# One gather in 96 moved from GpSimd to row-by-row transfers of SyncE

## What is computed

```python
h = (x @ W).reshape(n_nodes, Hh, Cc)
a_src = (h * att_src).sum(-1)
a_dst = (h * att_dst).sum(-1)
alpha = leaky_relu(a_src[src] + a_dst[dst])
m = jax.ops.segment_max(alpha, dst, num_segments=n_nodes)
e = jnp.exp(alpha - m[dst])
denom = jax.ops.segment_sum(e, dst, num_segments=n_nodes)
w = e / jnp.clip(denom, 1e-16)[dst]
out = jax.ops.segment_sum(w[:, :, None] * h[src], dst, num_segments=n_nodes)
```

## Time and profile before

| | |
|---|---|
| runs | 9,905.91, 9,902.95, 9,856.30 us; median 9,902.95 |
| profiled execution | 9,816.89 us, its span 9,815.1 us, mean granted TensorE clock 0.685 |
| PE busy | 5,477.6 us (56%), weight loads 3,976.8 (41%) |
| DVE busy | 5,141.6 us (52%) |
| POOL busy | 4,917.7 us (50%) |
| ACT busy | 2,159.9 us (22%) |
| DMA | 996.05 MB, mean 101 GB/s; GpSimd's queue 23.5% of 16 engines, SyncE's 9.6%, ScalarE's 2.0% |

### The profile page before, as it was taken

The page is one execution under the profiler, slowest core; times in us unless marked ns, Lnnn a source line. Parts: engine busy times, 40 slices in busy tenths (PEclk is TensorE's granted clock), DMA queues, the critical chain, the costliest instruction groups (busy, mean ns, idle before and its releaser), DMA issues. The chain is left out here.

```text
span 9815.1 us, 109787 instructions
## 1 busy us (share of the span) xinstructions
PE 5477.6 (56%) x24127; PEld 3976.8 (41%) x24128; DVE 5141.6 (52%) x15278; ACT 2159.9 (22%) x4026; POOL 4917.7 (50%) x5343
## 2 busy tenths in 40 slices
PE   5565555565655555555555555665555555555551
PEld 4344343344444434444444344553334443343330
DVE  3455454455546545554554445665545554554559
ACT  4111111121112412112111111351111111111113
POOL 2455555455453445545544455564444444444446
PEclk7666666666677766666666666786666666666665
DMA  7333333333333433333333333353333333333333
GB/s 195 89 98 96 96 96 96 94 99 98 94 99 85 135 94 100 98 94 100 98 94 94 93 99 96 113 170 94 96 96 96 96 96 95 95 95 96 93 91 106
DMA packets 489012, 996.05 MB, mean 101 GB/s; under 512 B 147014, under 2 KB 298808, under 8 KB 488342
## 3 DMA queue, kind: packets, MB, share of 16 engines
q0 software_dynamic: 227376, 635.50, 23.5%
q1 hardware_dynamic: 190836, 292.76, 9.6%
q10 hardware_dynamic: 70514, 65.01, 2.0%
HBM read 922.29 MB, written 70.57 MB: 101 GB/s over the span
## 5 line engine op out<-in xcount | busy, mean ns | idle before, releaser
L928 POOL DMA_INDIRECT e_rows<-table,e_loaded x4704 | 4462.1, 949 | 4482.0 <-PE e_p_mm L1001 2591.5
L1001 PE MATMUL e_p_mm<-e_rows,e_onehot 128*128 128x264 f32 x9408 | 2678.8, 447 | 0.0
L1001 PEld LDWEIGHTS e_p_mm<-e_rows,e_onehot 128*128 128x128 f32 x9408 | 2055.1, 224 | 438.7 <-issue 12.4
L1123 DVE TENSOR_TENSOR e_rows<-e_rows,e_p_e 128x1024 f32<-128x1024 f32 x1176 | 1418.4, 1206 | 0.0
L974 ACT ACTIVATE e_rows<-e_gap 128x64 f32<-128x64 f32 (+1 forms) x294 | 80.5, 274 | 5578.1 <-DVE e_gap L1281 5578.1
L1212 DVE TENSOR_TENSOR_SCAN e_fwd<-e_mask,e_p_one 64x128 f32<-64x128 bf16 (+1 forms) x294 | 121.7, 414 | 2138.4 <-remote 1724.3
L1115 DVE TENSOR_TENSOR e_onehot<-e_col,e_p_iota 128x512 f32<-128x512 f32 (+1 forms) x1470 | 951.0, 647 | 301.6 <-issue 292.6
L1059 PE MATMUL e_p_small<-ident,e_fwd 64*1 64x64 f32 (+1 forms) x588 | 114.1, 286 | 1657.0 <-DVE e_bwd L1213 996.1
L994 PE MATMUL e_p_mm<-e_xmsg,e_onehot 128*128 128x264 f32 x1764 | 888.6, 674 | 13.8 <-issue 13.8
L1246 DVE TENSOR_REDUCE e_adst<-e_p_one 128x64 f32<-128x192 f32 (+1 forms) x294 | 122.7, 417 | 1447.1 <-remote 1447.1
L1008 PE MATMUL e_p_one<-ad_parts,e_onehotT 128*128 x5586 | 536.8, 183 | 408.8 <-issue 407.2
(11 more groups left out here) (213 smaller groups left out, 6359.5 us busy)
## 6 DMA issues: line engine op xcount, KB each, us to landing
e_onehotT<-rel_rows SPq DMA_DIRECT2D x294, 608.0 KB
e_rows<-table,e_loaded POOLq DMA_INDIRECT x4704
table<-n_row ACTq DMA_DIRECT2D x196, 130.0 KB, 2.9
n_looprow<-table SPq DMA_DIRECT2D x196, 128.0 KB, 2.6
table<-n_row ACTq DMA_DIRECT2D x98, 132.0 KB, 1.9
n_node<-in_x_pad SPq DMA_DIRECT2D x98, 128.0 KB, 3.1
e_mask<-mask_rows SPq DMA_DIRECT2D x196, 64.0 KB
n_resrow<-in_x_pad SPq DMA_DIRECT2D x98, 128.0 KB, 2.6
```

The source lines that it names most:

```text
L928: pool.indirect_dma_start(rows[k][:, g, 0:TW], None, table[L], bass.IndirectOffsetOnAxis(ap=idx[k][:, g:g + 1], axis=0)).then_inc(s_gat[k] ...
L1001: ins = nc.tensor.matmul(p_mm[:, bass.ds(region, MW)], onehot[:, g, :], rows[k][:, g, :], start=False, stop=True, skip_group_check=True)
L1123: return nc.vector.tensor_tensor(feats, feats, p_e[:, g4, :].unsqueeze(3).to_broadcast([P, 4, H, C]), ALU.mult)
```

## The change

One gather in 96 leaves GpSimd's stream. Windows are counted in turns of six (TURN). In the last window of a turn GpSimd issues 15 gathers, and the 128 rows of that window's tile 15 are fetched by SyncE: in each of the first five windows of the turn it loads up to 26 node numbers (DIRECT) into registers and issues one transfer per row into a buffer of its own (`direct`; in the third layer a part of `as32`). In the sixth it waits for all of them and for the row buffer to be free, and copies `direct` into `rows[k][:, 15]` by one transfer in SBUF. ScalarE waits for that copy before its compact. SyncE's column load is issued one window ahead, the node numbers come with one small load per turn, and GpSimd's, SyncE's and ScalarE's loops are unrolled by six instead of three; TensorE and VectorE are as they were.

```diff
@@ -48,12 +48,14 @@
 BUFS = 3
+TURN = 6
+DIRECT = 26
...
-REGION_ROW, AD_ROW, WINDOW_ROW = 0, 32, 64
+REGION_ROW, AD_ROW, WINDOW_ROW, SRC_ROW = 0, 32, 64, 96
@@ -821,7 +823,9 @@
+    s_direct = [sem(f"e_direct{k}") for k in range(2)]
+    s_nodes, s_placed = (sem(f"e_{n}") for n in ("nodes", "placed"))
...
@@ -841,6 +845,7 @@
+            direct = sbuf(ph, tag + "direct", [P, TW], F32)[:] if TOPS else as32[:, 0:TW]
@@ -868,28 +873,29 @@
-            def walk(engine, body):
+            def walk(engine, body, unroll=BUFS):
...
-                for w in range(BUFS):
-                    at(w, w, 1, first=w == 0)
-                with engine.Fori(1, WINDOWS // BUFS) as i:
-                    for k in range(BUFS):
-                        at(i * BUFS + k, k, i + 1)
-                for w in range(WINDOWS // BUFS * BUFS, WINDOWS):
+                for w in range(unroll):
+                    at(w, w % BUFS, w // BUFS + 1, first=w == 0, turn=(0, w))
+                with engine.Fori(1, WINDOWS // unroll) as i:
+                    for r in range(unroll):
+                        at(i * unroll + r, r % BUFS, i * (unroll // BUFS) + (r // BUFS + 1), turn=(i, r))
+                for w in range(WINDOWS // unroll * unroll, WINDOWS):
                     at(w, w % BUFS, w // BUFS + 1)
@@ -919,25 +925,41 @@
-                def body(w, k, turns, ago, first):
+                def body(w, k, turns, ago, first, turn):
                     pool.wait_ge(s_idx[k], turns * 16)
-
-                    for g in range(G):
+                    by_row = turn is not None and turn[1] == TURN - 1
+
+                    for g in range(G - 1 if by_row else G):
...
-                walk(pool, body)
+                walk(pool, body, TURN)
...
-                def body(w, k, turns, ago, first):
-                    wait_apart(sp, st["cols"], ago(BUFS))
+                def load_columns(w, k):
                     sp.dma_start(loaded[k][:], col_dram[:, bass.ds(w * COL_W, COL_W)]).then_inc(s_idx[k], 16)
+
+                def load_nodes(i):
+                    sp.dma_start(off_row[SRC_ROW:SRC_ROW + 1, 0:P],
+                                 t["src_rows"][bass.ds(i * (TURN * G) + (TURN * G - 1), 1), :]).then_inc(s_nodes, 16)
+
+                def load_direct(first_row, n):
+
+                    nodes = words(sp, SRC_ROW, first_row, n, NODES_PAD - 1)
+                    for p, node in enumerate(nodes, first_row):
+                        sp.dma_start(direct[p:p + 1, :], table[L][bass.ds(node, 1), :]).then_inc(s_direct[p % 2], 16)
+
+                def body(w, k, turns, ago, first, turn):
+                    if first:
+                        load_columns(0, 0)
+                    if turn is not None and turn[1] == 0:
+                        load_nodes(turn[0])
                     wait_apart(sp, st["settled"], ago(BUFS))
...
-                walk(sp, body)
+                    if not (isinstance(w, int) and w == WINDOWS - 1):
+                        wait_apart(sp, st["cols"], ago(BUFS - 1))
+                        load_columns(w + 1, (k + 1) % BUFS)
+                    if turn is None:
+                        return
+                    i, r = turn
+                    if r == 0:
+                        wait_apart(sp, s_nodes, count(sp, (i + 1) * 16))
+                        wait_apart(sp, st["compact"], ago(1))
+                    if r < TURN - 1:
+                        load_direct(r * DIRECT, min(DIRECT, P - r * DIRECT))
+                    else:
+                        for parity in range(2):
+                            wait_apart(sp, s_direct[parity], count(sp, (i + 1) * (P // 2 * 16)))
+                        wait_apart(sp, s_mm[3], ago(BUFS))
+                        sp.dma_start(rows[k][:, G - 1, 0:TW], direct).then_inc(s_placed, 16)
+                walk(sp, body, TURN)
@@ -959,11 +997,17 @@
...
-                    act.wait_ge(s_gat[k], turns * (16 * G))
+                    gathered = turns * (16 * G)
+                    if turn is not None and k == TURN % BUFS + BUFS - 1:
+                        i, r = turn
+                        gathered = i * (2 * 16 * G - 16) + (16 * G if r < TURN - 1 else 2 * 16 * G - 16)
+                        if r == TURN - 1:
+                            wait_apart(act, s_placed, count(act, (i + 1) * 16))
+                    act.wait_ge(s_gat[k], count(act, gathered))
...
-                walk(act, body)
+                walk(act, body, TURN)
```

More of the change, by code:

```diff
@@ L93, in build_program @@
     zeros = sbuf(top, "zeros", [1, G * ADS_W], BF16)
-    off_row = sbuf(top, "off_row", [WINDOW_ROW + 1, TILES], I32)
+    off_row = sbuf(top, "off_row", [SRC_ROW + 1, TILES], I32)
     as32 = sbuf(top, "as32", [P, BLOCKS * 8], F32)
@@ L823, in build_program @@
     s_turn, s_done, s_step = (sem(f"e_{n}") for n in ("turn", "done", "step"))
-    per_layer = [*s_idx, *s_ld, s_turn, s_done, s_step]
+    s_direct = [sem(f"e_direct{k}") for k in range(2)]
+    s_nodes, s_placed = (sem(f"e_{n}") for n in ("nodes", "placed"))
+    per_layer = [*s_idx, *s_ld, s_turn, s_done, s_step, *s_direct, s_nodes, s_placed]
     s_clear = sem("e_clear")
@@ L869, in edge_phase, with at @@
             flat = lambda a: a[:].rearrange("o h g -> o (h g)")
-            def walk(engine, body):
-                def at(w, k, turns, first=False):
+            def walk(engine, body, unroll=BUFS):
+                def at(w, k, turns, first=False, turn=None):
                     regs = {}
@@ L881, in ago @@
                         return regs[n]
+                    place = () if unroll == BUFS else (turn,)
                     if isinstance(w, int):
-                        body(w, k, turns, ago, first)
+                        body(w, k, turns, ago, first, *place)
                     else:
-                        body(w if engine is nc.gpsimd else engine.snap(w), k, engine.snap(turns), ago, first)
-                for w in range(BUFS):
-                    at(w, w, 1, first=w == 0)
-                with engine.Fori(1, WINDOWS // BUFS) as i:
-                    for k in range(BUFS):
-                        at(i * BUFS + k, k, i + 1)
-                for w in range(WINDOWS // BUFS * BUFS, WINDOWS):
+                        body(w if engine is nc.gpsimd else engine.snap(w), k, engine.snap(turns), ago, first, *place)
+                for w in range(unroll):
[4 more added lines that the diff above has]
+                for w in range(WINDOWS // unroll * unroll, WINDOWS):
                     at(w, w % BUFS, w // BUFS + 1)
@@ L1359 @@
         "x_pad": x_pad, "edge_rows": np.ascontiguousarray(edge_rows), "edge_cols": np.ascontiguousarray(edge_cols),
-        "dst_rows": dst_rows, "tile_ends": np.concatenate([tile_first, tile_base, tile_last])[None],
+        "dst_rows": dst_rows, "src_rows": np.ascontiguousarray(src_pad.reshape(TILES, P)), "tile_ends": np.concatenate([tile_first, tile_base, tile_last])[None],
         "tile_base": np.ascontiguousarray(tile_base_rows.reshape(SG, P).T), "window_ends": window_ends,
```

## The result

The changed kernel takes **10,091.57 us** (median of four runs, 10,068.39 to 10,100.16), the kernel before 9,879.62 us beside it: **ratio 1.0218, 95% interval 1.0192 to 1.0245**, 2.2% slower. The forecast was 10,430 us, 5.3% slower, in a range of 9,840 to 11,100. The direction was right, the size more than twice too large.

What follows compares the result with a forecast made beforehand. Each window was taken as bound by its burst of gathers plus 9 to 10 us, TensorE's results becoming visible late. 9,816.9 - 48 + 576 = 10,345 us, put on the runs' median as 10,430 us; range 9,840 to 11,100.

Steps and rivals of the forecast that it cites:

- What bounds the kernel: Edge windows: TensorE's results become visible late during gathers, so a window is the burst (20.0 us) plus 9 to 10 us.
- Minus 48 us: GpSimd: one gather fewer per turn, 48 x 1.25 = 60 us, of which 0.8 counts; bounds 38 to 60 us.
- SyncE's free price: SyncE outside bursts: 0.54 us a row; with node numbers and window loads, 96 us of work per turn.
- The in-burst price: SyncE in a burst's slow stretch: 0.70 us an instruction, so 2.8 us a row, 5.2 times the free price.
- the sum's bounds for dearer rows: SyncE's shortfall per turn: rows of 0.63 us give 24 us (1,152 us in all), of 0.91 us give 59 (2,800).
- Plus 576 us: SyncE fits 84 of 96 us per turn; the 12 us debt delays loads, repaid one for one over 48 turns.
- Where the loads' delay is absorbed: ACT idles 18.4 us before L974, so it absorbs the first delays, but not a backlog over all of a turn.
- The rival TensorE held back: SyncE's stream delays TensorE's results, lengthening VectorE's wait before L1212: 720 us on top, 10,575 us; chance 0.13.
- Hidden: Rival: SyncE keeps its free pace in bursts, 96 of 180 us fit, faster at 9,855 us; chance 0.17.
- a draw: Rival: rows are slowed, but a debt of 0 to 1 us a turn eats the credit, 9,903 us; chance 0.12.
- one at a time: Rival: SyncE's queue takes a row only when the last has landed, 1.6 us each, 12,350 us; chance 0.04.
- What the next profile would show: Signs: rows 0.54 us apart between bursts, 2 to 3 inside; L942 10 us and more late; ACT waiting before L956.

Runs made afterwards that it cites:

- c15_plain: Changed kernel without the row transfers: direct filled by two plain transfers of 64 rows per turn, 15 gathers in one window of six; ratio 0.9935 to the kernel before.
- f_fixed: Changed kernel with the 128 row transfers per turn at fixed addresses, one instruction a row instead of three, node numbers not loaded; ratio 1.0229.
- g6: Changed kernel with one more wait: SyncE issues a window's rows only after all of that window's own gathers; ratio 1.0328.
- n_instr: c15_plain plus three idle SyncE instructions (satisfied semaphore waits) per row, 384 a turn, no row transfers; ratio 1.0185.
- fg6: f_fixed with the added wait of g6, so a window's 26 transfers go out after its own gathers; ratio 0.9997.
- n_gap: n_instr with the added wait of g6, so a window's 78 idle instructions come after its own gathers; ratio 0.9970.
- t9: Changed kernel with turns of nine windows instead of six, 16 rows in each of the first eight; ratio 1.0091.
- g9: t9 with the added wait of g6: a window's 16 rows issued only after its own gathers have landed; ratio 0.9993.
- g12: g9 with turns of twelve windows, 12 rows in each of eleven; ratio 0.9967.
- g12b: g12 with no rows in a layer's first two windows, the rest of the first turn taking 15 rows; ratio 0.9969.
- p_start: Kernel before, with a layer's second and third window's columns loaded only when the gathers of the window before have landed; ratio 0.9943.
- g9b: g9 with no rows in a layer's first two windows, 22 in each of the next six; ratio 1.0028.
- h_half: Changed kernel with only 64 rows per turn fetched by row, 13 in a window, the other 64 by one plain transfer; ratio 1.0055.
- n_one: n_instr with one idle instruction per row instead of three, 26 in a window; ratio 1.0103.
- l_act_c15: l_act without the row transfers, as in c15_plain; ratio 1.0085.
- l_act: Changed kernel with a window's four loads issued by ACT instead of SyncE, which issues only the rows; ratio 1.0159.
- s6: Changed kernel with one more wait: SyncE starts a window's rows only after VectorE's scan of the window before; ratio 1.0180.
- s16_rows: Changed kernel with all 16 gathers kept in every window and the on-chip copy dropped; the 128 rows per turn are fetched but unread; ratio 1.0261.

## Why the prediction came out as it did

- **What bounds the kernel** was right: the results of TensorE become visible late in a burst, and the window is the burst plus 9 to 10 us. In the changed kernel a period is as long as before for each kind of release; only the kinds are otherwise mixed.
- **Minus 48 us** for the gather: borne out in size, 64 us (39 to 89) in c15_plain, though more than the gathers changed there.
- **SyncE's free price** was too high. 0.54 us a row came from L942 to L943, and L942 writes 128 partitions; a row of one partition is 0.41 us apart. 128 x 0.13 = 17 us a turn, more than the 12 us that the sum found missing: with the right price its own capacity of 84 us would have held 79. The in-burst price was too high as well: 1.9 us on average, against 2.8, though single rows took 3.8. The 26 words took 1.7 us at the median and up to 5.5, against 2.1. In the sum's bounds for dearer rows the 84 us of capacity should have grown with the row's price: 18 and 38 us short instead of 24 and 59.
- **Plus 576 us is the step that failed**: "12 us short", a debt over all of a turn, paid by "time without gathers, about one for one". SyncE was not short. With 0.41 us a row it needs 79 us a turn, and at 1.9 us in a burst it has 54 + 126 x 0.41/1.9 = 81 us without any allowance. Within a turn a lateness does appear: the loads of the third window go out 5.7 us into their burst at the median, single ones in the fourth and fifth up to 30 us; but in the sixth SyncE is idle for some 19 us, and nothing is carried to the next turn. What costs in place of the debt is that SyncE is at work inside the bursts at all: f_fixed has the loads in time in every window of its turns (0.7 to 1.1 us before the burst at the median) and a ratio of 1.0229. A debt of the kind forecast is seen in g6, where the rows do not fit: there the loads of a turn's six windows go out 2, 4, 15, 20, 27 and 25 us into the burst.
- **Where the loads' delay is absorbed** was misread too. ACT's 18.4 us of idle time before L974 lie behind the lookups, not ahead of them. From the issue of e_onehotT's load to ACT's lookup there are 5.3 us (median in the changed kernel), so a few us of lateness reach ACT at once: 1,158 us of waiting. It costs less than that, because VectorE mostly waits for TensorE meanwhile; g6 shows the price when it does not.
- **The rival TensorE held back** named the mechanism that the runs found, and was given 0.13. Its price, 5.9 us lengthened in 240 windows and half hidden, was a guess of 720 us and is 2.6 times too high. The delay from L1095 to e_fwd grew by 2.7 us, over 294 windows 805 us, of which at most some 277 reach the end. Its sign, "VectorE's wait before L1212 longer while L942 is on time", is just what f_fixed shows. Its argument that the release comes in the middle of the window was right also: it is the windows that stop at e_inf that increased.
- **Hidden, a draw, one at a time**: none. SyncE's slow row is on average just the 1.9 us at which the first was to decide: the work fits into SyncE's time, as that rival says, and yet the kernel is slower, so fitting was not the question. Rows 0.41 us apart rule out one at a time. The Trainium skill's rule on small transfers (DMA: Bandwidth & Descriptors, Rules for kernel authors) pointed the right way for another reason: the estimate of 256 us a turn from its fixed part (which that page gives for transfers that GpSimd issues) did not come, and n_instr loses nearly as much with no small transfer at all.
- **What the next profile would show**: rows quick outside and slow inside, 15 gathers at 1.25 us, ACT waiting before L994 and GpSimd's wait for matmuls up from 2,592 to 2,805 us all came. "L942 10 us and more late" came in 13 of 279 windows only; that sign would have told the debt from the rest.

So most of the loss comes from a mechanism other than the one forecast. Shown is that SyncE's instructions cost by their place in a burst (f_fixed against fg6, n_instr against n_gap, and less cleanly t9 against g9), that neither row transfers nor late loads are needed, and that TensorE's first result reaches VectorE later the more of them there are. The table has the mean delay from L1095 to e_fwd and ACT's whole wait before its first lookup, both counted in the traces, for all runs:

| kernel | delay, us | ACT waits, us | ratio |
|---|---|---|---|
| g12 | 4.3 | 229 | 0.9967 |
| g12b | 4.3 | 145 | 0.9969 |
| p_start | 4.4 | 172 | 0.9943 |
| before | 4.4 | 101 | 1 |
| c15_plain | 4.8 | 160 | 0.9935 |
| g9 | 4.8 | 483 | 0.9993 |
| g9b | 4.8 | 354 | 1.0028 |
| n_gap | 5.0 | 293 | 0.9970 |
| fg6 | 5.2 | 518 | 0.9997 |
| t9 | 5.9 | 183 | 1.0091 |
| h_half | 6.1 | 205 | 1.0055 |
| n_one | 6.2 | 212 | 1.0103 |
| f_fixed | 7.5 | 179 | 1.0229 |
| n_instr | 7.8 | 258 | 1.0185 |
| l_act_c15 | 0.2 | 1,034 | 1.0085 |
| l_act | 1.2 | 1,077 | 1.0159 |
| g6 | 4.7 | 4,724 | 1.0328 |
| s6 | 5.6 | 1,850 | 1.0180 |
| s16_rows | 6.1 | 1,303 | 1.0261 |
| after | 7.1 | 1,158 | 1.0218 |

In the rows above the last six, where ACT waits for 518 us at most, the ratio goes roughly with the delay. In the last six ACT waits for over 1,000 us (in the two l_act runs it issues the loads itself), and the delay alone does not order them: s16_rows loses 2.6% with a delay at which n_one and h_half lose 1.2 to 1.7% above c15_plain, and s6 more than twice what its delay would give. So late loads have a part of their own. An estimate: h_half, n_one, f_fixed and n_instr lose 0.8 to 1.2% above c15_plain for each us of added delay; that would make 1.9 to 2.8% of the 2.85% of the changed kernel, and 1.4 to 2.0% of the 2.6% of s16_rows, and leave the rest to the late loads.

What TensorE and SyncE share while gathers run is not shown. Nor does any run settle how the loss of the changed kernel divides between this delay and ACT's late loads, because none removed only the second without adding work elsewhere or changing the rows; nor why fg6 lies 0.6% above c15_plain, of which transfers between bursts, by n_gap, would be somewhat under half, within the intervals.

## What to carry to other kernels

An idle queue is not free because its engine waits: ask at what moment its instructions fall and who is due a result then. Here the same 128 transfers cost 3.0% or 0.6% above a kernel without them (f_fixed and fg6 against c15_plain), depending on whether they go out while GpSimd's gathers run, and one wait moves them. Take the price of a small instruction from the row whose shape is nearest, and find the slack of a load from its issue to its first reader, not from the reader's idle time elsewhere. And look first at the work that sets the end: parting a burst of 48 gathers, by one wait, was worth about as much as taking 48 gathers away.

## What the runs showed of the hardware that was not expected

- Instructions without any transfer slow down as well: SyncE's satisfied semaphore waits took 0.70 us each in a burst of gathers and 0.017 us after it, and 78 of them in a window made the kernel 2.5% slower than without.
- They delay another engine: VectorE's scan started 7.8 us after the modelled end of the transpose that it needs on average, against 4.8 us without them.
- GpSimd's own pace does not suffer, 1.25 us a gather in the timelines of all of them.
- Delaying a layer's second and third window's gathers until the ones before had landed made the kernel 0.57% (0.31 to 0.84) faster.
